# A decoder layer with a mixture of experts on one core: gates one tile per iteration, expert weights and scatters inside the last cross attention, two dense tiles at the end

## What is computed

```
x = x + self_attention(layernorm(x))            # 16 heads, causal, rotated q and k
x = x + cross_attention(layernorm(x), ctx)      # 16 heads, 722 context rows of 384 features
h = layernorm(x)
gates = softmax(h @ gate_w.T + gate_b)          # 8 experts
top_gates, top_idx = top_k(gates, 2)
expert_out = einsum('bsh,eoh->bseo', h, expert_w) + expert_b
x = x + sum over the 2 picked experts of top_gates * expert_out
```

## Time and profile before

| | us |
|---|---|
| median of 3 runs | 1348.55 |
| lowest, highest | 1347.22, 1349.49 |
| the profiled execution | 1345.71 |
| its span | 1344.0 |

### The profile page before, as it was taken

The page is one execution under the profiler, slowest core; times in us unless marked ns, Lnnn a source line. Parts: engine busy times, 40 slices in busy tenths (PEclk is TensorE's granted clock), DMA queues, the critical chain, the costliest instruction groups (busy, mean ns, idle before and its releaser), DMA issues.

```text
span 1344.0 us, 43383 instructions
## 1 busy us (share of the span) xinstructions
PE 1219.1 (91%) x19183; PEld 805.2 (60%) x19183; DVE 835.3 (62%) x1458; ACT 642.9 (48%) x942; POOL 725.3 (54%) x686
## 2 busy tenths in 40 slices
PE   4789899999999999999999999999997844688898
PEld 4456667675767667676757676766765642344433
DVE  4657576777767686767776776768575863311155
ACT  4236465646555554656465555555564632032300
POOL 1436566575757666665757575766665616200041
PEclk8799999999999999999999999999998866699999
DMA  8010601101010101010010101010103334234364
GB/s 288 1 41 2 252 9 42 39 11 47 3 48 2 48 2 48 9 42 24 26 41 9 47 3 48 2 48 4 47 9 112 104 109 158 71 110 141 126 204 145
DMA packets 43429, 84.74 MB, mean 63 GB/s; under 512 B 3293, under 2 KB 14869, under 8 KB 43245
## 3 DMA queue, kind: packets, MB, share of 16 engines
q1 hardware_dynamic: 40044, 71.48, 16.3%
q0 software_dynamic: 3200, 10.49, 2.3%
HBM read 56.00 MB, written 25.95 MB: 61 GB/s over the span
## 4 chain that ended last, share of the span: by engine, by line
PE 82%; DMA 4%; DVE 4%; POOL 3%; issue 3%; ACT 2%; SPq 1%; ACTq 0%; DVEq 0%; POOLq 0%
PE psum L273 53%; PE psum L832 7%; PE psum L930 6%; PE psum L915 5%; DMA prob<-xs_scratch 3%; PE psum L850 2%; PE psum L809 2%; PE psum L801 1%; POOL xs_scratch L638 1%; DMA bank<-in_L_attn_Wv 1%; PE psum L456 1%; DVE c_most L1158 1%; PE psum L765 1%; PE psum L817 1%; DVE xT L1073 1%
## 5 line engine op out<-in xcount | busy, mean ns | idle before, releaser
L1336 POOL TENSOR_TENSOR bank<-prob,bank 128x1200 f16<-128x1200 f32 x128 | 314.9, 2470 | 206.7 <-ACT bank L1019 206.7
L1158 DVE TENSOR_REDUCE c_most<-psum 100x4 f32<-100x1444 f32 x128 | 211.5, 1653 | 20.8 <-PE psum L915 18.7
L273 PE MATMUL psum<-bank,cT 128*128 128x512 f16 (+1 forms) x864 | 198.6, 379 | 0.0
L273 PE MATMUL psum<-cT,bank 128*128 128x361 f16 x1152 | 195.9, 321 | 0.0
L1010 ACT ACTIVATE prob<-psum 128x1200 f32<-128x1200 f32 x128 | 150.0, 1172 | 60.6 <-PE psum L930 56.4
L1019 ACT ACTIVATE bank<-prob 128x1200 f16<-128x1200 f32 x128 | 151.6, 1197 | 1.5
L273 PEld LDWEIGHTS psum<-cT,bank 128*128 128x128 f16 x1152 | 105.9, 99 | 65.1 <-issue 3.5
L273 PEld LDWEIGHTS psum<-bank,cT 128*128 128x128 f16 (+1 forms) x864 | 85.2, 101 | 88.0 <-issue 4.1
L1001 ACT ACTIVATE cv<-psum 128x512 f16<-128x512 f32 x96 | 57.4, 598 | 153.5 <-PE psum L273 151.9
L1126 DVE SCALAR_TENSOR_TENSOR bank<-psum,b_part,bank 128x361 f16<-128x361 f32 x128 | 74.4, 591 | 86.7 <-ACT bank L991 86.7
L991 ACT ACTIVATE bank<-psum,b_part 128x361 f16<-128x361 f32 x128 | 72.1, 563 | 108.6 <-PE psum L273 108.6
(11 more groups left out here) (225 smaller groups left out, 2009.6 us busy)
## 6 DMA issues: line engine op xcount, KB each, us to landing
c_raw<-in_ctx SPq DMA_DIRECT2D x16, 960.0 KB
xs_scratch<-y_kept SPq DMA_DIRECT2D x1, 6912.0 KB, 21.6
prob<-xs_scratch SPq DMA_DIRECT2D x27, 256.0 KB, 2.8
ys_scratch<-bank SPq DMA_DIRECT2D x27, 256.0 KB, 2.0
cT<-in_L_ffn_expert_w SPq DMA_DIRECT2D x4, 1024.0 KB, 5.4
cv<-in_L_ffn_expert_w SPq DMA_DIRECT2D x4, 1024.0 KB, 5.5
x_in<-in_x SPq DMA_DIRECT2D x16, 200.0 KB
x_scratch<-x_out SPq DMA_DIRECT2D x16, 200.0 KB
```

The lines of the kernel that those rows point to most:

```text
L273: last = pe.matmul(out_ap, a(pa), b(pb), start=(i == 0 and j == 0), stop=(i == len(pairs) - 1 and j == 2))
L1158: dve.tensor_reduce(c_most[:, hf], score[0:L, :, 0:HC], AXIS.X, ALU.max).then_inc(max_done, 1)
L1336: pool.tensor_tensor(prob16[o % 2][:, (2 + part) * PT:(3 + part) * PT], prob[:, part], prob16[o % 2][:, part * PT:(part + 1) * PT], ALU.su ...
```

## The change

- There are 1400 routed rows (batches 0 to 13) in 11 tiles, the last of 120 rows, and two dense tiles, batches 14 and 15, of 100 rows each. There are 29 slot tiles.
- A tile's load, norm, `FX` and `FL` stand in the iteration in which its last batch has just been stored: tiles 0 to 9 in iterations 3, 4, 5, 7, 8, 9, 10, 12, 13, 14 (steps 2, 3, 5, 7), tile 10 late in 14. The norm goes to a DRAM tensor, `xn_scratch`, and is read back, four buffers in turn, for the scatters.
- The routing is cut into four parts at the ends of steps 16 to 19 of iteration 14. In that iteration `TP` moves from step 11 to step 7.
- Iterations 15 and 16 have lists of their own. `LAST_STEPS` holds the cross attention, all 32 `FW`, the placing in step 2 and the 11 scatter pairs `SC`. Experts 0, 1 and 2 are loaded into the place of their own split weights in iteration 14; there ScalarE writes the first high part only when all four parts are transposed.
- `END_STEPS` holds the slot tiles, `ST` the transposes and `SM` the product, with the tail of batch 15 and the gates of batch 15 in between. A slot tile's load is issued when the transposes four tiles earlier are read.
- The dense tiles, all 8 experts, come after the slot tiles with the 13 biases.

The diff, cut to its core:

```diff
-EARLY = 10
-ROUTE_STEP = 15
-X2_STEP = next(h for h, step in enumerate(STEPS) if "TP" in step) + 1
-LATE = TT - EARLY
-SLOT_TILES = 2 * EARLY + E - 1
+EARLY = 11
+EARLY_ROWS = B * L - 2 * L
+LATE = 2
+TILES = EARLY + LATE
+SLOT_TILES = (2 * EARLY_ROWS + E * (P - 1)) // P
 SLOTS = SLOT_TILES * P
-DENSE_FIRST = 2
-EXTRA_CHUNKS = {
-    B - 1: {h: ([f"FG0"] if h == 2 else []) + ([f"FX{h - 4}"] if 0 <= h - 4 < EARLY else []) +
-            ([f"FL{h - 5}"] if 0 <= h - 5 < EARLY else []) + (["FR"] if h == ROUTE_STEP + 1 else []) +
-            [f"FW{i // KD}{i % KD}" for i in (2 * h - 10, 2 * h - 9) if 0 <= i] for h in range(2, LAST_STEP + 1)},
-
-    -1: {7: ["BV0", "BV1"]},
-    B: {2: ["FW72", "FW73"],
-        LAST_STEP: [f"F{w}{t}" for t in range(EARLY, TT) for w in "XL"]},
-}
+
+
+def tile_rows(t):
+
+    if t < EARLY:
+        return t * P, min(P, EARLY_ROWS - t * P)
+    return EARLY_ROWS + (t - EARLY) * L, L
+
+
+def turn(t):
+
+    return (sum(tile_rows(t)) - 1) // L + 2
+
+
+def moved(steps, name, to):
+    return [[c for c in step if c != name] + ([name] if h == to else []) for h, step in enumerate(steps)]
...
+GATE_EXTRA = {11: ["FS10"], 12: ["FN10"], 14: ["FX10"], 15: ["FL10"], 16: ["RT00", "RE0"], 17: ["RT01"], 18: ["RT02"],
+              19: ["RT03", "RP"]}
...
+LAST_STEPS = [
+    ["low3a", "A0", "max_A0", "low3b", "FW00", "FW01", "FW02", "FW03"],
+    ["B0", "max_B0", "FW10", "FW11", "FW12", "FW13"],
+    ["MX0", "PV3", "FR"],
+    ["T0a", "exp0a", "scale_heads"],
+    ["T0b", "exp0b", "SC0", "high0a", "TT"],
+    ["A1", "max_A1", "low0a", "high0b", "FW20", "FW21", "FW22", "FW23"],
+    ["B1", "max_B1", "low0b", "TP"],
+    ["MX1", "SC1", "FW30", "FW31", "FW32", "FW33"],
+    ["T1a", "exp1a", "PV0", "SC2"],
+    ["T1b", "exp1b", "high1a", "FW40", "FW41", "FW42", "FW43"],
+    ["A2", "max_A2", "low1a", "high1b"],
+    ["B2", "max_B2", "low1b", "FS11", "SC3"],
+    ["MX2", "FW50", "FW51", "FW52", "FW53", "FN11"],
+    ["T2a", "exp2a", "PV1", "SC4"],
+    ["T2b", "exp2b", "high2a", "FX11"],
+    ["A3", "max_A3", "low2a", "high2b", "FL11", "FW60", "FW61", "FW62", "FW63"],
+    ["B3", "max_B3", "low2b", "SC5"],
+    ["MX3", "SC6", "FW70", "FW71", "FW72", "FW73"],
+    ["T3a", "exp3a", "PV2", "SC7"],
+    ["T3b", "exp3b", "high3a", "high3b", "SC8", "SC9", "SC10"],
+]
+END_EXTRA = {2: ["PV3", "scale_heads"], 5: ["TT"], 6: ["TP"], 9: ["FS12"], 10: ["FN12"], 11: ["FX12"], 12: ["FL12"],
+             13: ["RT10", "RE1"], 14: ["RT11"], 15: ["RT12"], 16: ["RT13"]}
+END_STEPS = [["low3a", "low3b", "ST0", "ST1"]] + [
+    ([f"ST{j + 2}"] if j + 2 < SLOT_TILES else []) + [f"SM{j}"] + END_EXTRA.get(j + 1, []) for j in range(SLOT_TILES)]
+def steps_of(n):
+    if n == B - 1:
+        return LAST_STEPS
+    if n == B:
+        return END_STEPS
+    every = [list(step) for step in (moved(STEPS, "TP", 7) if n == B - 2 else STEPS)]
+    for t in range(EARLY - 1):
+        if turn(t) == n:
+            for h, name in ((2, "FS"), (3, "FN"), (5, "FX"), (7, "FL")):
+                every[h].append(f"{name}{t}")
+    extra = GATE_EXTRA if n == B - 2 else {2: ["FG0"], 7: ["BV0", "BV1"]} if n < 0 else {}
+    for h, names in extra.items():
+        every[h] += names
+    return every
...
+        raw_home = (None, None, None, "c", "T", "v", "T", "v")
+        raw_e = [(bank[:, e * KD * 2 * D:(e + 1) * KD * 2 * D].bitcast(F32) if raw_home[e] is None else
+                  raw_space[raw_home[e]]).rearrange("p (o h) -> p o h", o=KD) for e in range(E)]
...
+        def load_again(sp, t):
+            at, n = tile_rows(t)
+            if t >= 4:
+                sp.wait_ge(scattered[t % 4], 32 * (t // 4))
+            sp.dma_start(y_again[t][0:n], xn_dram[at:at + n]).then_inc(again_loaded[t % 4], 16)
...
+        def pe_slots(pe, j):
+            if j < 4:
+                pe.wait_ge(exp_done, 2 * GROUPS * B)
+            else:
+                pe.wait_ge(slot_out, j - 3)
+            if j == 0:
+                pe.wait_ge(experts_ready, 1)
+            pe.wait_ge(chunk_out, its[B].done(f"ST{j}"))
+            e = pe.value_load(expert_i[0:1, j:j + 1], min_val=0, max_val=E - 1)
+            split3(pe, psum[:, j % 4, 0:D], [(lambda p, k=k: slotsT[j % 3][:, p, k],
+                                              lambda p, k=k: wT_all[:, bass.ds(e, 1), k, p].rearrange("p e f -> p (e f)"))
+                                             for k in range(KD)]).then_inc(slot_ready, 1)
...
+            pool.wait_ge(again_loaded[t % 4], 16 * (t // 4 + 1))
             for i in range(2):
-                pool.indirect_dma_start(xs_dram[:, :], bass.IndirectOffsetOnAxis(ap=slot_i[:, i, t:t + 1], axis=0),
-                                        y_norm[t], None).then_inc(scattered, 16)
+                pool.indirect_dma_start(xs_dram[:, :], bass.IndirectOffsetOnAxis(ap=slot_i[0:n, i, t:t + 1], axis=0),
+                                        y_again[t][0:n], None).then_inc(scattered[t % 4], 16)
...
-                ffn_loads(sp, it)
+                last_loads(sp, it)
                 return
+            if n == B:
+                end_loads(sp, it)
+                return
+            turned = [t for t in range(EARLY - 1) if turn(t) == n]
+            for t in turned:
+                load_y(sp, t)
+            if n == B - 2:
+                sp.wait_ge(chunk_out, it.done("SV"))
+                for e in range(3):
+                    load_expert(sp, e)
             if it.tail:
                 sp.wait_ge(chunk_out, it.done("TP"))
                 sp.dma_start(x2_dram[n - 1], x_out[:]).then_inc(x2_stored, 16)
-            if n == B:
-                for t in range(EARLY, TT):
-                    load_y(sp, t)
+            for t in turned:
+                store_y(sp, t)
             if n < B - 2:
                 sp.wait_ge(chunk_out, it.done("SO"))
                 load_ctx(sp, n + 2)
                 sp.wait_ge(chunk_out, it.done("OP"))
                 load_x(sp, n + 2)
             if n == B - 2:
-                sp.wait_ge(chunk_out, it.done("OP"))
-                sp.dma_start(g_raw, gW).then_inc(g_loaded, 16)
-                sp.dma_start(e_bias, eb).then_inc(g_loaded, 16)
-                sp.wait_ge(slots_zeroed, 16)
-                for t in range(EARLY):
-                    load_y(sp, t)
-        def ffn_loads(sp, it):
-            for h in range(len(STEPS)):
-                if h == 0:
-                    sp.wait_ge(chunk_out, it.all_before())
-                    load_expert(sp, 0)
-                if h == 4:
-                    sp.wait_ge(chunk_out, it.done("PV3"))
-                    load_expert(sp, 1)
-                if h == X2_STEP:
+                load_y(sp, EARLY - 1)
+                sp.wait_ge(chunk_out, it.done("SO"))
+                load_expert(sp, 3)
+                store_y(sp, EARLY - 1)
+                sp.wait_ge(y_stored, 16 * EARLY)
+                sp.wait_ge(chunk_out, it.done(f"FL{EARLY - 1}"))
+                for t in range(4):
+                    load_again(sp, t)
+        def last_loads(sp, it):
+            sp.wait_ge(chunk_out, it.all_before())
+            load_expert(sp, 4)
+            sp.wait_ge(chunk_out, it.done("PV3"))
+            load_expert(sp, 5)
+            sp.wait_ge(chunk_out, it.done("TP"))
+            sp.dma_start(x2_dram[B - 2], x_out[:]).then_inc(x2_stored, 16)
+            load_again(sp, 4)
+            load_y(sp, EARLY)
+            load_again(sp, 5)
+            sp.wait_ge(chunk_out, it.done("FW43"))
+            load_expert(sp, 6)
+            load_again(sp, 6)
+            sp.wait_ge(chunk_out, it.done("FW53"))
+            load_expert(sp, 7)
+            for t in range(7, EARLY):
+                load_again(sp, t)
+        def end_loads(sp, it):
+            all_scattered(sp)
+            sp.wait_ge(chunk_out, its[B - 1].done("FW33"))
+            for j in range(4):
+                load_slots(sp, j)
+            for j in range(SLOT_TILES):
+                if j + 4 < SLOT_TILES:
+                    sp.wait_ge(chunk_out, it.done(f"ST{j}"))
+                    load_slots(sp, j + 4)
+                if j >= 2:
+                    store_slots(sp, j - 2)
+                if j == 4:
+                    sp.wait_ge(prob_low, 2 * GROUPS * B)
+                    sp.dma_start(e_bias, eb).then_inc(e_bias_loaded, 16)
+                if j == 7:
                     sp.wait_ge(chunk_out, it.done("TP"))
-                    sp.dma_start(x2_dram[B - 2], x_out[:]).then_inc(x2_stored, 16)
-                e = (h - 8) // 2 + 2
-                if h >= 8 and h % 2 == 0 and e < E:
-                    sp.wait_ge(chunk_out, it.done(f"FW{e - 2}{KD - 1}"))
-                    load_expert(sp, e)
+                    sp.dma_start(x2_dram[B - 1], x_out[:]).then_inc(x2_stored, 16)
+                if j == 8:
+                    load_y(sp, TILES - 1)
+            for j in range(SLOT_TILES - 2, SLOT_TILES):
+                store_slots(sp, j)
```

(20 more changed lines are left out.)

374 lines of the change are left out of this document (183 added, 191 removed).

## The result

The changed kernel takes 1286.47 us (median of 4 runs, 1285.15 to 1287.90) against 1347.88 us for the kernel before beside it (4 runs, 1345.78 to 1349.49). The ratio is 0.9545, 95% interval 0.9528 to 0.9563. Its profiled execution took 1286.48 us with a span of 1284.7. The total came out as forecast; the parts did not.

What follows compares the result with a forecast made beforehand. TensorE was taken to bound middle iterations, chains of waits the last cross attention, GpSimd's scatters the stretch after. Terms +11 - 66.9 - 5.5 - 1.2 = -62.6 took 1345.7 to 1283, forecast 1285 with the median's 2.8; range 1264 to 1308.

Steps and rivals of the forecast that it cites:

- Part 1: Gates in iterations 3 to 14: +11 us, from 11 tiles at 0.79 and 2.3 for the routing.
- The rival of dear gates: Full iterations: a stall of 2 us per gate tile, +30 instead of +11, 1304 us; chance 0.10.
- Part 2: First scores of batch 15 to first slot matmul: 146.9 us falls to 80, bounds 70 and 95.
- The attention, 65: Last cross attention: 80.6 us falls to 65 without routing (7.9), expert wait and gate tiles; bounds 55 and 81.
- The rival that the attention is not shortened: Last cross attention: weight chunks ahead of each second maximum keep it at 81 us, total 1301; chance 0.15.
- the sum from below: Last cross attention: VectorE's maxima, weight chunks, joins and waits built up per group, four times 15 is 60 us.
- The last scatter, 72: GpSimd's queue: group 2's low half at 57 us, then six scatter pairs at 2.5 us, ending at 72.
- the ring of four buffers: Scatters and reloads: buffers run in step with late scatter landings, costing 52 us (1337) or more; chance 0.03.
- The routing meets more subtractions: Routing pieces on VectorE stall on three GpSimd subtractions, 6 us more before batch 15's first maximum, 1291; chance 0.10.
- Part 3: Slot tiles: 101 us falls to 95.4, 29 tiles at 3.03 with earlier loads plus extras; bounds 93 and 116.
- The rival that the load stays the clock: Slot tiles: loads still set the pace, 21 us more, total 1306; chance 0.13.
- Part 4: The end, after the slot tiles: 65.5 us falls to 64.3, with 16 dense tiles and 13 biases; bounds 62 and 70.

Runs made afterwards that it cites:

- e3: The changed kernel without its 22 scatters, reloads kept, so it does not compute the layer: 1275.50 us.
- e9: The changed kernel with each of the 22 scatters replaced by a plain GpSimd store to fixed rows, so not the layer: 1277.29 us.
- e10: The changed kernel without scatters and with all 32 weight chunks moved behind the last cross attention, so not the layer: 1290.46 us.
- e8: The changed kernel with ScalarE's copy of the first turned slot tile ahead of its two last probability copies: 1283.62 us.
- e1: The kernel before with only the slot-tile load moved ahead of the output wait and store: 1328.08 us.
- e2: The changed kernel with the slot loads put back behind the store that waits for the tile's output: 1305.26 us.

## Why the prediction was right, and where its parts were off

**Part 1, gates, +11: half.** The 0.79 a tile held (0.75), and none is hidden. Iteration 14, with two tiles and most of the routing, took 2.7 us more (66.57 against 63.91) where 3.9 were forecast; the routing's rest fell behind the first scores and belongs to part 2. What brought +11 down to +5.5 is mostly the 4 us by which the kernel before was slower in iterations 6 to 13 with no more than 0.4 us in any one gap. One middle iteration was read and taken for all. The rival of dear gates is out.

**Part 2, 80: 89.5.** Two terms were mis-sized, one was missing.
- *The attention, 65.* It took 83.75. 13.0 of the difference are the scatters (e3, e9), which stood in no term: I had asked what the attention costs the scatters' queue and not what the scatters cost the attention. Without them it is 70.75, within 6 of the forecast. The two waits behind the routing, 2.72 + 3.44 = 6.2, are about that, for the sum had taken the routing's 7.9 off whole; no run takes these waits away alone. The rival that the attention is not shortened had the right size, 81. Its mechanism, weight chunks ahead of the second maxima, is real but did not make the miss: the waits are there (4.45 and 3.16 us), yet all 32 chunks together cost 11.2 us (e10), and the sum from below already held them at 0.64 each, 20.5.
- *The last scatter, 72.* It ended at 78.4: group 2's low halves were done at 63.2, not 57, since the attention was late. The twelve scatters themselves took 15.0, as worked out, and the ring of four buffers never held GpSimd.
- *From the slot load to the slot matmul.* The load went out at 80.7 and took 2.9 us or more, so it landed no sooner than 83.6; the transposes started at 83.75, straight behind the last turned scores. So the scatters' chain and the attention ended together, and the first slot matmul hung on both. From the landing the forecast had 2 us; it was 5.7 from the transposes' start, for ScalarE had an exponential and two probability copies in front of the slot tile's (e8: 2.2 less).
- *The routing meets more subtractions*, 6 us, had a chance of 0.10 as a case of its own. It happened, with two meetings and 4.0 us in place of three and 6. By the Trainium skill's rule (SBUF — State Buffer, "Who interferes with whom") each of the two instructions waits until GpSimd's ends; the trace agrees, 2.13 and 2.39 us in place of 0.25.

**Part 3, 95.4: 93.1.** Right in its cause, shown from both sides by e1 and e2. The rival that the load stays the clock is what e2 measures, 110.0. The forecast's extras were 2 us too many.

**Part 4, 64.3: 66.0.** Close; no run looked into it.

The total stood by luck: +5.5 us too much in part 1 and +2.3 in part 3 covered most of the 9.5 us missing in part 2 and the 1.7 in part 4. The 2.8 us put on top for the median (1283 + 2.8 is 1285.8, given as 1285) covered nearly 3 us more, for the changed kernel's profiled execution lies at its median. The sum was better than its terms.

## What to carry to other kernels

Before work is overlapped, ask in both directions: what the host stage costs the guest and what the guest costs the host. Indirect DMAs from GpSimd are not free guests beside a stage of many short matmuls; put them beside longer ones (the transposes here showed no gap), or measure the stage without them. And look first for the cheap order on a queue: a load behind a store that waits for an output cost 17 us here, and moving three lines took it back.
